# An audio tower on one core: norms, routing and output in three tiles of 128 tokens, values as three packed tiles, new orders of the steps

## What is computed

```python
h = tok(x)                                            # (64, 92, 128)
def attention(x):                                     # 8 heads of 64, per sample
    q, k, v = split(x @ w_qkv.T)
    attn = softmax(q @ k.T * scale)                   # 92 x 92 for each head
    attn = einsum('bhij,hg->bgij', attn, reattn_w)    # heads mixed
    a = normalised over the 8 heads, * ln_g + ln_b
    return (a @ v) @ w_out.T + b_out
def ffn(x):
    scores = softmax(x @ gate_w.T); top 2 of 8 experts, weights renormalised to combine
    y = sum over experts of combine * (relu(x @ w1 + b1) @ w2 + b2)
    return y + relu(x @ sw1 + sb1) @ sw2 + sb2
h = h + attention(layernorm(h))
h = h + ffn(layernorm(h))
```

## Time and profile before

| | |
|---|---|
| Median of the runs | 714.72 us |
| Profiled execution | 717.34 us, of it 715.5 us span |
| TensorE busy | 646.5 us, 90% |
| VectorE, ScalarE, GpSimd busy | 506.8, 415.8, 406.2 us |
| Mean granted TensorE clock | 0.964 of full |

### The profile page before, as it was taken

The page is one execution under the profiler, slowest core; times in us unless marked ns, Lnnn a source line. Parts: engine busy times, 40 slices in busy tenths (PEclk is TensorE's granted clock), DMA queues, the critical chain, the costliest instruction groups (busy, mean ns, idle before and its releaser), DMA issues.

```text
span 715.5 us, 18159 instructions
## 1 busy us (share of the span) xinstructions
PE 646.5 (90%) x5880; PEld 578.4 (81%) x5880; DVE 506.8 (71%) x1543; ACT 415.8 (58%) x1382; POOL 406.2 (57%) x495
## 2 busy tenths in 40 slices
PE   4687979999999999999999999999999999986666
PEld 3576869888898889888888988898888888875565
DVE  2845576868777877878687778878787877765532
ACT  2265557565675757575656757575656657563312
POOL 1534446657493847656574938476565848374603
PEclk9799889999999999999999999999999999999877
DMA  6000020030202020110202020201202020302020
GB/s 206 1 23 1 23 86 23 13 104 1 95 21 95 21 95 21 67 50 1 98 18 95 21 95 21 95 21 45 71 1 95 21 97 1 97 2 96 0 90 17
DMA packets 16634, 36.69 MB, mean 51 GB/s; under 512 B 1440, under 2 KB 13664, under 8 KB 14560
## 3 DMA queue, kind: packets, MB, share of 16 engines
q1 hardware_dynamic: 16608, 36.35, 16.0%
HBM read 33.14 MB, written 3.20 MB: 51 GB/s over the span
## 4 chain that ended last, share of the span: by engine, by line
PE 64%; DVE 21%; issue 5%; POOL 5%; ACT 2%; DMA 2%; POOLq 0%; SPq 0%; DVEq 0%; ACTq 0%
PE ps_fill L394 13%; PE ps_mix L599 11%; PE ps_fill L395 11%; PE ps_fill L396 11%; PE ps_dots L588 7%; DVE xn L941 6%; PE ps_av L607 5%; PE ps_fill L543 5%; POOL rstd L1179 2%; DVE stats L927 2%; DVE key L970 2%; DVE aT L1022 2%; DVE hot L973 1%; DMA spread<-weights 1%; DVE mv L932 1%
## 5 line engine op out<-in xcount | busy, mean ns | idle before, releaser
L466 POOL TENSOR_TENSOR act_split_lo<-act,act_split_hi 128x736 fp32r<-128x736 f32 (+1 forms) x80 | 128.2, 1606 | 33.3 <-ACT act_split_hi L805 33.3
L1147 POOL TENSOR_TENSOR sum<-sq 92x384 f32<-92x384 f32 x64 | 64.5, 1007 | 117.5 <-ACT sq L747 117.5
L739 ACT ACTIVATE ex<-ps_dots,negmax 128x92 f32<-128x92 f32 x384 | 123.4, 333 | 13.3 <-DVE negmax L1003 13.3
L599 PE MATMUL ps_mix<-mixk,probs 128*92 128x128 f32 x768 | 101.9, 285 | 16.3 <-DVE aT L1024 16.0
L599 PEld LDWEIGHTS ps_mix<-mixk,probs 128*92 128x92 f32 x768 | 89.6, 166 | 25.0 <-issue 17.5
L1100 DVE SCALAR_TENSOR_TENSOR act<-ps_fill,b_neg,spread 128x368 f32<-128x368 f32 x128 | 72.9, 591 | 49.5 <-PE ps_fill L396 42.3
L1141 POOL TENSOR_TENSOR probs<-ex,rinv 128x552 f32<-128x552 f32 x64 | 71.2, 1113 | 30.0 <-DVE rinv L1009 30.0
L588 PE MATMUL ps_dots<-xT,yT 128*64 128x92 f32 x1536 | 74.9, 247 | 7.6 <-ACT ex L739 3.9
L747 ACT ACTIVATE sq<-ps_mix 92x768 f32<-92x768 f32 x64 | 51.4, 804 | 48.1 <-PE ps_mix L599 48.0
L588 PEld LDWEIGHTS ps_dots<-xT,yT 128*64 128x64 f32 x1536 | 63.4, 137 | 18.3 <-issue 11.3
L739 ACT ACTIVATION_READ_ACCUMULATOR ex<-ps_dots,negmax 128x1 f32 x384 | 78.1, 203 | 0.0
(11 more groups left out here) (160 smaller groups left out, 1697.9 us busy)
## 6 DMA issues: line engine op xcount, KB each, us to landing
spread<-weights SPq DMA_DIRECT2D x16, 1472.0 KB, 6.2
xin<-in_x SPq DMA_DIRECT2D x16, 320.0 KB
out<-ostage SPq DMA_DIRECT2D x16, 160.0 KB
act<-w_raw SPq DMA_DIRECT2D x2, 576.0 KB, 7.3
xin<-in_x SPq DMA_DIRECT2D x16, 52.0 KB
qkv<-qk_raw SPq DMA_DIRECT2D x1, 512.0 KB, 5.3
out<-ostage SPq DMA_DIRECT2D x16, 24.0 KB
spread<-tok_raw SPq DMA_DIRECT2D x1, 256.0 KB, 3.6
```

Of the source, the lines that this page charges most:

```text
L466: eng.tensor_tensor(lo, act1[:, two, :], hi.bitcast(F32), ALU.subtract).then_inc(units_ready, 1)
L599: last = pe.matmul(ps_mix[0:N, c // HALF, o:o + 128], probs[:, (s - 1) % 2, c, :], mixk[:, :, :].rearrange("p g i -> p (g i)"), start=True ...
L739: last = act.activation(ex[:, s % 2, c, :], ps_dots[:, c // HALF, o:o + N], ACT.Exp, bias=negmax[:, c:c + 1], accum_out=sums[:, s % 2, c:c ...
L1147: pool.tensor_tensor(sum4[:, :, :, :], sq[:, :, 0:4, :], sq[:, :, 4:8, :], ALU.add)\
```

## The change

1. Norms, routing and output work on the group's 368 tokens as three tiles of 128 columns (the buffers hT, h2T, fT, xT_split, x2T are widened to 384 columns, the last 16 set to zero once). TH, TH2, TX, TX2, CT and OT are three transposes in place of four; the statistics, the aggregates and xn three operations in place of four; RT six matmuls in place of eight. The output leaves in two DMAs of 2 x 128 and 112 rows.
2. The values are three steps in place of four. XS gets four more copies on GpSimd, which pack the high and the low part of the normed tokens into xV: tile t holds the 92 tokens at place t in rows 0 to 91 and a third of the fourth sample's tokens in rows 96 to 127. V0, V2 and V3 each multiply a whole tile; ScalarE empties each with two copies (92 rows, then 28 or 32 rows to the slot SPLIT_SLOT). V1, which VectorE emptied, is gone. PLACE says where each of the four samples lies, V_READ what `av` waits for.
3. All lists of steps are new: SETUP, ORDER_0, STEPS, ORDERS_END. With one fill fewer in a pass (33 in place of 34) the banks fall differently.

```diff
+TILES = 3
+R = 128
+WP = TILES * R
+PLACE = (0, 3, 1, 2)
+V_TILES = {"V0": (0, 0), "V2": (1, 2), "V3": (2, 3)}
+V_READ = {0: [("V2", 1)], 1: [("V3", 1)], 2: [("V0", 1)], 3: [("V0", 1), ("V2", 0), ("V3", 0)]}
+SPLIT_SLOT = 1
...
 STEPS = [
-    ("dots", 0), ("max", 0), ("mix", 0), ("sq", 0), "Z7", "Z6", ("exa", 0), ("av", 0), "Z2", ("ev", 0), "Z5",
-    ("exb", 0), ("rstd", 0), ("inv", 0), ("scale", 0), "Z4", "Z3", ("dots", 1), ("max", 1), "XE", ("av", 1),
-    ("mix", 1), "H2", ("ev", 1), "Z0", ("exa", 1), ("sq", 1), ("exb", 1), "XO", "OP", "H1", "shift", ("inv", 1),
-    "Z1", ("dots", 2), ("max", 2), ("rstd", 1), "H3", ("scale", 1), ("exa", 2), "TK", ("exb", 2), "TH2", "Z8", "TH",
-    ("mix", 2), ("dots", 3), "NH2", "NH", ("av", 2), ("sq", 2), "TX2", "H0", "V2", "V3", ("inv", 2), ("max", 3),
-    ("exa", 3), "RT", "H4", ("rstd", 2), "R2", ("scale", 2), "R3", "TX", ("ev", 2), "YF", ("mix", 3), "CT", "XS",
-    "Y4", ("av", 3), ("sq", 3), "Y7", ("exb", 3), "Y3", "Y2", ("inv", 3), "V1", "Y6", "Y1", ("rstd", 3), "Y0", "Y5",
-    "OT", ("scale", 3), "V0", ("ev", 3), "hold", "BS",
+    ("dots", 0), ("max", 0), ("av", 0), ("ev", 0), ("mix", 0), ("exa", 0), "Z5", "Z3", "Z2", ("sq", 0), ("exb", 0),
+    "Z6", ("inv", 0), "XE", ("dots", 1), ("rstd", 0), ("max", 1), ("scale", 0), "Z8", "Z0", "Z1", ("exa", 1), "XO",
+    ("mix", 1), ("exb", 1), ("av", 1), ("inv", 1), ("dots", 2), ("sq", 1), ("ev", 1), ("max", 2), "H0", "Z7", "OP",
+    ("rstd", 1), ("scale", 1), "shift", "H1", "TK", "TH2", "Z4", ("exa", 2), "TH", ("mix", 2), ("av", 2), "NH2",
+    "NH", ("exb", 2), "H3", ("dots", 3), "H2", "TX2", ("sq", 2), ("max", 3), "V2", ("exa", 3), "H4", ("inv", 2),
+    "RT", "R2", ("rstd", 2), "V3", "R3", ("scale", 2), "YF", "TX", "CT", ("ev", 2), ("mix", 3), "XS", "Y6", "Y5",
+    "Y3", ("sq", 3), "Y2", "hold", ("exb", 3), "Y1", ("inv", 3), "OT", ("av", 3), ("ev", 3), "Y4", ("rstd", 3), "Y7",
+    ("scale", 3), "Y0", "V0", "BS",
 ]
...
 ORDERS_END = [[
-    ("dots", 0), "Z8", ("max", 0), ("exa", 0), ("exb", 0), ("mix", 0), "Z7", "Z3", "Z4", ("dots", 1), ("max", 1),
-    ("sq", 0), ("exa", 1), ("rstd", 0), ("av", 0), ("exb", 1), "Z1", "Z2", ("scale", 0), ("inv", 0), ("ev", 0), "Z6",
-    "Z5", "H1", ("dots", 2), ("av", 1), ("mix", 1), ("max", 2), "H3", ("ev", 1), ("inv", 1), ("sq", 1), ("exa", 2),
-    "OP", "Z0", ("exb", 2), "TH2", ("dots", 3), "shift", ("rstd", 1), ("max", 3), ("exa", 3), ("scale", 1), "NH2",
-    "H2", "V3", "H0", ("av", 2), "TX2", "H4", ("mix", 2), ("sq", 2), ("inv", 2), "RT", "R2", ("exb", 3), "R3",
-    ("rstd", 2), ("scale", 2), ("ev", 2), "YF", "CT", "hold", "V2", ("mix", 3), "OT", ("sq", 3), ("rstd", 3),
-    ("inv", 3), ("av", 3), ("scale", 3), ("ev", 3),
+    ("dots", 0), ("mix", 0), ("max", 0), "Z5", ("sq", 0), "Z2", "Z4", "Z0", ("exa", 0), ("av", 0), ("exb", 0),
+    ("inv", 0), ("ev", 0), ("dots", 1), ("rstd", 0), ("scale", 0), "H2", "Z6", "Z1", ("av", 1), ("max", 1),
+    ("mix", 1), ("ev", 1), ("exa", 1), ("sq", 1), ("exb", 1), "Z7", ("inv", 1), "H0", "OP", ("dots", 2), ("max", 2),
+    ("rstd", 1), "Z8", ("scale", 1), ("exa", 2), "TH2", "Z3", ("exb", 2), "NH2", ("av", 2), "H1", ("mix", 2),
+    ("dots", 3), ("max", 3), ("ev", 2), "H3", ("sq", 2), "TX2", "H4", ("inv", 2), ("exa", 3), "RT", "V3", ("exb", 3),
+    "R2", ("rstd", 2), "R3", ("scale", 2), "YF", "shift", "CT", ("mix", 3), ("sq", 3), "V2", "OT", ("inv", 3),
+    ("rstd", 3), ("av", 3), "hold", ("scale", 3), ("ev", 3),
 ], [
-    "Z8", ("mix", 0), "Z2", "Z1", ("sq", 0), ("av", 0), ("ev", 0), "Z7", "Z0", "H4", ("rstd", 0), ("scale", 0), "Z6",
-    "Z5", ("av", 1), "H0", ("ev", 1), "Z4", "H3", "H2", "Z3", "OP", "H1", "TH2", "NH2", "TX2", "RT", "R2", "R3",
-    "YF", "hold", "CT", "OT",
+    "Z8", ("mix", 0), ("sq", 0), ("av", 0), ("ev", 0), "Z5", "H4", "Z1", "Z0", ("rstd", 0), ("scale", 0), "H0", "Z4",
+    "Z6", ("av", 1), ("ev", 1), "Z7", "OP", "H2", "Z2", "TH2", "Z3", "NH2", "H3", "TX2", "RT", "R2", "R3", "H1",
+    "YF", "CT", "OT", "hold",
 ], [
-    "Z8", "Z1", "Z2", "Z0", "Z3", "H4", "Z6", "H0", "Z5", "H1", "Z4", "H2", "Z7", "H3", "YF", "OT",
+    "Z8", "H4", "Z3", "Z2", "Z0", "Z1", "Z5", "H1", "Z4", "Z6", "H0", "H2", "Z7", "H3", "YF", "OT",
 ]]
...
 SETUP = [
-    "XE", "XO", "prepT", "TK", "prepB", "pA0", "pA1", "TH", "prepW", "NH", "prepO", "TX", "pM", "prepX", "V0",
-    "Y2", "pD", "prepE", "Y3", "Y0", "Y1", "Y5", "Y7", "XS", "Y4", "Y6", "V1", "BS",
+    "XE", "XO", "prepT", "prepW", "TK", "TH", "prepO", "NH", "pA0", "pA1", "TX", "pM", "Y7", "Y4", "Y3", "Y1",
+    "prepB", "Y6", "Y0", "XS", "Y5", "Y2", "pD", "prepX", "prepE", "V0", "BS",
 ]
...
                 if step == "OT":
                     wait_emptied(sp, "OT", G)
-                    for rows in (slice(0, SPREAD_ROWS), slice(SPREAD_ROWS, N)):
-                        sp.dma_start(out_rows[rows, bass.ds(SLOTS * (G - 2), SLOTS), :],
-                                     ostage[rows, :, :]).then_inc(stored, 16)
+                    sp.dma_start(out_tiles[:, :, bass.ds(G - 2, 1), :], ostage[:, 0:2, :].unsqueeze(2))\
+                      .then_inc(stored, 16)
+                    sp.dma_start(out_rows[2 * R:W, bass.ds(G - 2, 1), :], ostage[0:W - 2 * R, 2:3, :])\
+                      .then_inc(stored, 16)
...
-                        rows = yT[:, 2 * s + c // HALF, c % HALF, :, :].rearrange("p h i -> p (h i)")
+                        rows = yT[:, 2 * PLACE[s] + c // HALF, c % HALF, :, :].rearrange("p h i -> p (h i)")
                         for r in range(0, 128, DH):
                             last = pe.matmul(ps_dots[r:r + DH, c // HALF, o:o + N], rows[:, r:r + DH],
-                                             xT[:, N * s:N * s + N], start=True, stop=True)
+                                             xT[:, N * PLACE[s]:N * PLACE[s] + N], start=True, stop=True)
...
                     if kind == "av":
-                        vs = (s - 2) % SLOTS
-                        wait_emptied(pe, f"V{vs}", G - 1)
+                        for values_step, back in V_READ[s]:
+                            wait_emptied(pe, values_step, G - back)
...
-                    "Y0": [("TX", 0)],
+                    first_scored(G): [("TX", 0)],
...
                     last.then_inc(done, 1)
                 elif step in ("TH", "TH2"):
-                    src = hT if step == "TH" else h2T
-                    transposes(step, G, [(ps[0:N, 128 * s:128 * s + 128], src[:, s, :], ident)
-                                         for s in range(SLOTS)])
+                    src = hT_tiles if step == "TH" else h2T_tiles
+                    transposes(step, G, [(ps[:, R * t:R * t + R], src[:, R * t:R * t + R], ident)
+                                         for t in range(TILES)])
                 elif step in ("TX", "TX2"):
                     src = xn[step == "TX2"]
-                    transposes(step, G, [(ps[:, N * s:N * s + N], src[:, s, :], ident[0:N, 0:N])
-                                         for s in range(SLOTS)])
+                    transposes(step, G, [(ps[:, R * t:R * t + R], src[:, t, :], ident) for t in range(TILES)])
                 elif step[0] == "Y" and step != "YF":
                     products(ps[:, 0:W], [a[:, int(step[1]), :] for a in A], [m[:, 0:W] for m in xT_split])\
                         .then_inc(done, 1)
                 elif step[0] == "V":
-                    o = N * int(step[1])
-                    products(ps[0:N, :], [m[:, o:o + N] for m in xT_split], [w[:, :, :] for w in wvT])\
+                    if step == "V0":
+                        pe.wait_ge(xV_ready, g + 1)
+                    products(ps[:, :], [m[:, V_TILES[step][0], :] for m in xV], [w[:, :, :] for w in wvT])\
                         .then_inc(done, 1)
...
                 elif step == "RT":
-                    for s in range(SLOTS):
-                        x_hi, x_lo = [m[:, N * s:N * s + N] for m in x2T]
-                        o = 2 * E * s
-                        pe.matmul(ps[0:N, o:o + 2 * E], x_hi, gate_both[:, :], start=True, stop=False)
-                        last = pe.matmul(ps[0:N, o:o + E], x_lo, gateT[0], start=False, stop=True)
+                    for t in range(TILES):
+                        x_hi, x_lo = [m[:, R * t:R * t + R] for m in x2T]
+                        o = 2 * E * t
+                        pe.matmul(ps[:, o:o + 2 * E], x_hi, gate_both[:, :], start=True, stop=False)
+                        last = pe.matmul(ps[:, o:o + E], x_lo, gateT[0], start=False, stop=True)
                     last.then_inc(done, 1)
...
                 elif step in ("V0", "V2", "V3"):
-                    empty(step, G, v_sb[:, int(step[1]), :], ps[0:N, :])
+                    tile, slot = V_TILES[step]
+                    rows = min(COPY, N - COPY * tile)
+                    wait_filled(act, step, G)
+                    act.activation(v_sb[:, slot, :], ps[0:N, :], ACT.Copy)
```

(20 more changed lines are left out.)

116 lines of the change are left out of this document (60 added, 56 removed), and 3 rows, old and new, of the table ORDER_0.

## The result

The changed kernel takes 722.15 us (median of four runs, 719.92 to 723.32), the kernel before 714.58. The ratio is 1.0105, 95% interval 1.0078 to 1.0133: 1% slower. The forecast was 711.7 with a range of 690 to 722.

What follows compares the result with a forecast made beforehand. TensorE was taken to fill nearly all of a pass, with VectorE's routing next in line. Passes +4.5, setup -3.5, first groups -2 and tail -2 gave -3: 714.3 us profiled, 711.7 as a median, range 690 to 722.

Steps and rivals of the forecast that it cites:

- The pass: Each of thirteen passes takes 39.9 us in place of 39.5, about +0.35; in all +4.5 us, between 0 and +8.
- GpSimd's queue through probs: GpSimd's work up to probs ends 28.6 us after a pass's first `dots`, one unit more than before, holding VectorE's routing.
- 1.4 ahead of CT: TensorE waits 1.4 us in each pass ahead of CT for the end of R3.
- 0.9 ahead of `mix`(3): TensorE waits 0.9 us in each pass ahead of `mix`(3), released by aT.
- TensorE's own work: Value steps, transposes, RT and block changes together take 1.7 us less of TensorE a pass, between 0.5 and 2.1.
- The value steps: One of four goes, saving 0.76 us of TensorE a pass; 128 stationary columns cost nothing, at worst the whole 0.76.
- The count of held operations: VectorE's two-SBUF-input routing operations wait for GpSimd's current instruction to end; at least four would take 0.4 us or more.
- holds no worse than now: Rival: only two routing operations held, `mix`(3) starts at 30.5, a pass takes 38.7 or less, 694 us; chance 0.27.
- The clock: Rival: TensorE's two waits count as one, half rate costs 1.9 us a pass, 736 us; within 0.15 for all slower cases.
- Setup and the first groups: Before group 2: setup gains 3.5 us, between 0 and 5; groups 0 and 1 gain 2, between -1 and 4.
- Tail: Groups 15 and 16 and the output gain 2 us, between -2 and 4.
- Copies on GpSimd: Four more packing copies take 1.2 us in all, 1.9 at the slower rate, and cost the pass nothing.

Runs made afterwards that it cites:

- e4: Changed kernel with the low parts of H2 and H3 on GpSimd cut to 8 of 368 columns, the rest left out of the computation; 686.95 us, ratio 0.9632.
- e12: Changed kernel with two steps moved in the steady order: H1 ahead of Z8, H3 behind shift, everything still computed; 691.29 us, ratio 0.9679.
- e2: Changed kernel with the list STEPS of the kernel before, V1 taken out; 715.62 us, ratio 1.0013.
- e8: Changed kernel with SETUP and ORDER_0 of the kernel before, V1 left out; 747.08 us, ratio 1.0488.
- e1: Changed kernel with eight extra matmuls, results overwritten, ahead of CT's wait in groups 2 to 14; 700.56 us, ratio 0.984.
- e7: Changed kernel with four extra matmuls, results overwritten, ahead of CT's wait in groups 2 to 14; 703.31 us, ratio 0.9875.

## Why the prediction was wrong

**The pass.** Forecast 39.9, measured 39.7 where the clock holds. Its steps one by one: RT's wait 0.45, measured 0.54; GpSimd's queue through probs until t = 28.6, measured 329.80 - 301.45 = 28.35; 1.4 ahead of CT, measured 1.38 to 1.39; 0.9 ahead of `mix`(3), measured 0.64. VectorE's first routing operation came at t = 23.45 (23.5), the end of the routing at 30.58 (30.5). TensorE's own work fell by 1.6 us (39.5 less 1.0 of idle time before, 39.7 less 2.75 after), forecast 1.7. RT's share of it was no saving: six matmuls at 0.11 us in place of eight at 0.08. The value steps kept their gain: V0 costs 0.69 us with 128 columns of stationary data (341.59 to 342.28), 0.76 before.

The count of held operations was wrong, though. The forecast wanted at least four of 0.4 us or more, and two were held; two was the mark of its rival "holds no worse than now", which would have given a pass of 38.7. It is not the number of held operations that sets the end of the routing but the end of GpSimd's queue, and that the forecast had right. e4 and e12 show that this is the cause behind CT's wait. The Trainium skill, SBUF — State Buffer, Who interferes with whom, says that a VectorE instruction with two SBUF inputs contends with a GpSimd instruction that reads SBUF. The runs agree where such an operation was held, 2.06 us in place of 0.18; three such operations in the same chain passed in 0.18 to 0.25 us beside GpSimd's sums, so the forecast's reading that every one is held is not borne out.

**The clock: the step that failed.** The forecast kept the clock at 1.0 and made the fall a rival inside the 0.15 for slower. That rival put its point between 2.2 and 4.1 us of waiting, which left two waits of 2.3 us in sum on the edge, and held against itself that CT runs in between. Both arguments failed: 2.03 us in two parts (1.39 and 0.64) brought the clock down in 11 of 13 passes, e2's 1.05 in 6. The rows it leaned on were single long waits at the tail; no row of before showed two short ones close together, and the bound should have been left open downward. The size was nearly right, 1.9 us a fall against 1.55. Thirteen passes at +0.2 and eleven falls at 1.55 are the +19.4 us. (e2 shows that even an order with waits of 0.4 and 0.7 isn't safe.)

**Setup and the first groups.** TX came at 17.87 as forecast (18), the first max at 32.14 (33 to 35), 5.1 us in place of 3.5. From there to group 2 the gain was 70.17 - 64.56 = 5.6 us, and I had 2, between -1 and 4. This term was mis-sized. I had counted steps, and neither the order nor the clock: over this stretch the mean clock rose from 0.85 to 0.89. e8 shows that with packed values the orders of the setup and of group 0 decide about more than 20 us; what each of these brought of the 5.6 stays open.

**Tail.** Gain 4.3, forecast 2. CT's wait in group 15 fell from 2.17 to 1.83, that of group 16's `mix`(0) from 4.09 to 1.49, and that `mix`(0) keeps its clock behind the shorter wait (1.52 us in place of the 2.47 of the earlier trace rows).

**The sum.** The passes lost 14.9 us more than forecast and the ends won 7.5 us more, so two errors of opposite sign brought the forecast nearer to the measured time than either deserves. Another 2.6 us is the difference between profiled execution and median, which I took over from the kernel before; the changed kernel's profiled execution lies at its median. With the measured ends and no falls, the forecast would have been 15 - 2.7 = 12 us below before, about 702; e1 and e7, whose profiled passes have no falls, took 700.6 and 703.3. The case that the prediction took for likeliest was right about the wait, and it missed the second effect of the same wait.

**Copies on GpSimd.** 0.41 and 0.27 us, two of each, 1.4 us and free in the passes, as forecast (1.2); not free in a setup with V0 ahead (e8).
